# Expert rows in units of 64 (blocks of 256, 384 and 320), with TensorE's loop over pairs of experts written out four times

## What is computed

```python
gate = jnp.einsum('bsd,ed->bse', x, Wg) + routing_bias
_, top_idx = jax.lax.top_k(gate, K)            # K = 4 of E = 8
mask = jax.nn.one_hot(top_idx, E, dtype=gate.dtype).sum(-2)
masked_gate = jnp.where(mask > 0, gate, -jnp.inf)
weights = jax.nn.softmax(masked_gate, axis=-1) * mask
out = _swiglu(x, Ws1, Ws2, Ws3)
h1 = jnp.einsum('bsd,ehd->ebsh', x, W1)
h2 = jnp.einsum('bsd,ehd->ebsh', x, W2)
eo = jnp.einsum('ebsh,edh->ebsd', jax.nn.sigmoid(h1) * h1 * h2, W3)
out = out + jnp.einsum('ebsd,bse->bsd', eo, weights)
```

## Time and profile before

| | us |
|---|---|
| runs shown | 993.48 (median), 991.69, 5251.34 |
| the profiled execution | 993.76 |
| its span in the profile | 992.0 |

### The profile page before, as it was taken

The page is one execution under the profiler, slowest core; times in us unless marked ns, Lnnn a source line. Parts: engine busy times, 40 slices in busy tenths (PEclk is TensorE's granted clock), DMA queues, the critical chain, the costliest instruction groups (busy, mean ns, idle before and its releaser), DMA issues.

```text
span 992.0 us, 25401 instructions
## 1 busy us (share of the span) xinstructions
PE 975.7 (98%) x8054; PEld 798.5 (80%) x8054; DVE 560.8 (57%) x1411; ACT 508.4 (51%) x1250; POOL 545.4 (55%) x513
## 2 busy tenths in 40 slices
PE   9998999999999999999999999999999999999997
PEld 4665666788887888888788878788888887887886
DVE  4998787745544454545444545454455444554686
ACT  3676444355454554455445545445455454554366
POOL 4554027757633347633956016076888880785873
PEclk9999999999999999999999999999999999999999
DMA  6859024355532333353244214218773882785785
GB/s 223 248 143 185 1 60 131 99 173 131 163 108 78 104 92 97 98 171 96 59 145 138 57 48 124 58 49 187 127 101 68 125 132 53 106 127 88 103 149 143
DMA packets 168051, 113.86 MB, mean 115 GB/s; under 512 B 113596, under 2 KB 160191, under 8 KB 166848
## 3 DMA queue, kind: packets, MB, share of 16 engines
q0 software_dynamic: 29808, 58.37, 27.5%
q1 hardware_dynamic: 115888, 33.15, 16.1%
q10 hardware_dynamic: 22304, 21.76, 6.6%
HBM read 47.09 MB, written 43.12 MB: 91 GB/s over the span
## 4 chain that ended last, share of the span: by engine, by line
PE 87%; POOL 5%; DVE 3%; issue 2%; DMA 1%; ACT 1%; SPq 1%; ACTq 0%; DVEq 0%; POOLq 0%
PE psA L1073 53%; PE psB L1104 22%; PE psA L1021 5%; POOL y_sum L759 4%; PE psA L1104 2%; PE psB L1107 2%; DMA y_sum<-rows_by_place,place 1%; PE psC L1055 1%; DVE g_lo L1509 1%; PE psB L1034 1%; PE psC L1048 1%; SPq L519 1%; PE psC L1175 0%; DVE psC L1499 0%; DVE work L1291 0%
## 5 line engine op out<-in xcount | busy, mean ns | idle before, releaser
L874 ACT ACTIVATE sil<-psA 128x256 f32<-128x256 f32 (+1 forms) x456 | 178.3, 398 | 281.6 <-PE psA L1073 253.7
L759 POOL DMA_INDIRECT y_sum<-rows_by_place,place x128 | 200.0, 1563 | 82.5 <-issue 39.0
L1499 DVE SCALAR_TENSOR_TENSOR g<-psA,sil 128x256 f32<-128x256 f32 (+1 forms) x160 | 72.0, 450 | 306.1 <-ACT sil L874 305.7
L1073 PE MATMUL psA<-xb_odd,work 128*128 128x256 f16 x1980 | 221.1, 273 | 0.4 <-issue 0.4
L1073 PEld LDWEIGHTS psA<-xb_odd,work 128*128 128x128 f16 x1980 | 193.0, 98 | 24.1 <-issue 1.4
L1104 PE MATMUL psB<-work,g_hi 128*128 128x256 f16 x1260 | 211.5, 273 | 0.8 <-DVE g_lo L1509 0.3
L1073 PE MATMUL psA<-xb,work 128*128 128x256 f16 x1782 | 199.0, 273 | 2.2 <-issue 1.3
L1073 PEld LDWEIGHTS psA<-xb,work 128*128 128x128 f16 x1782 | 173.4, 98 | 24.4 <-issue 4.0
L1499 DVE SCALAR_TENSOR_TENSOR psC<-psA,sil 128x256 f32<-128x256 f32 (+3 forms) x296 | 133.0, 449 | 77.2 <-ACT sil L874 71.2
L1104 PE MATMUL psB<-work,g_lo 128*128 128x256 f16 x630 | 171.8, 273 | 0.0
L706 POOL DMA_INDIRECT rows_by_place<-y_rows,place x96 | 95.1, 990 | 136.6 <-DMA rows_by_place<-y_rows,place 122.5
(11 more groups left out here) (176 smaller groups left out, 1036.0 us busy)
## 6 DMA issues: line engine op xcount, KB each, us to landing
stage<-wpack POOLq DMA_DIRECT2D x9, 2176.0 KB, 8.9
rows_by_place<-eb ACTq DMA_DIRECT2D x57, 256.0 KB
work<-xT SPq DMA_DIRECT2D x7, 512.0 KB, 6.0
work<-half_beta SPq DMA_DIRECT2D x6, 512.0 KB, 4.6
work<-x_tok POOLq DMA_DIRECT2D x6, 512.0 KB, 6.8
rows_by_place<-eb ACTq DMA_DIRECT2D x6, 384.0 KB
rows_by_place<-zeros SPq DMA_DIRECT2D x1, 2112.0 KB, 12.9
rows_by_place<-y_rows,place POOLq DMA_INDIRECT x128, 2.5
```

What stands on the lines that cost most here:

```text
L759: pool.indirect_dma_start(out=y_sum[:, n, :], out_offset=None, in_=xs, in_offset=bass.IndirectOffsetOnAxis(ap=place[:, k, n:n + 1], axis=0 ...
L874: act.activation(sil[r0:r0 + n, c % SLOTS, 0:T], psA[0:n, chunk_bank(c, T), 0:T], ACT.Silu, scale=1.0 / (XS * WS)).then_inc(silu_ready, 1)
L1073: last = pe.matmul(dst, W[:, ws, k, ci, :], xb[slot][:, KD * xs_ + k, 0:T], start=(k == 0 and n == 0), stop=(k == KD - 1 and n == 2))
L1499: dve.scalar_tensor_tensor(gated_rows(g, c, 0, n, T), src, 1.0 / (XS * WS), sil[r0:r0 + n, c % SLOTS, 0:T], ALU.mult, ALU.mult).then_inc(g ...
```

## The change

Sizes are counted in units of 64 rows. An expert with `u` units (at least 4; from 5 to 11 units it is rounded up to a multiple of 4) is cut as before into an inner loop of 256 blocks, and behind it there can be a block of 384 (`wide`, when bit 1 of `u` is set) and a block of 320 (`short`, when bit 0 is set). The 256 blocks are the units that are left. With the rows above, `u` is 45, 48, 17, 34, 21, 23, 46, 25, in all 259, and the blocks (256 + 384 + 320) are 10+0+1, 12+0+0, 3+0+1, 7+1+0, 4+0+1, 3+1+1, 10+1+0, 5+0+1: 54 of 256, 3 of 384 and 5 of 320. A 320 block moves 384 rows in and out (`J = 3` groups, `-(-T // P)`), has three groups in `down`, and 320 columns in `up`.

```diff
+UNIT = P // 2
+TM = TL - UNIT
...
+        def units_of(eng, units):
+
+            short, wide = eng.snap(units & 1), eng.snap((units >> 1) & 1)
+            return eng.snap(units >> 2), wide, short
...
-            with eng.If(full > 0):
-                with eng.Fori(0, turns) as i:
-                    run(TB, first + 2 * i, rows_from(2 * i), 2 * w)
-                    left = eng.snap(full - 2 * i)
-                    with eng.If(left > 1):
-                        run(TB, first + (2 * i + 1), rows_from(2 * i + 1), 2 * w + 1)
-            with eng.If(odd > 0):
+            with eng.Fori(0, turns) as i:
+                run(TB, first + 2 * i, rows_from(2 * i), 2 * w)
+                left = eng.snap(full - 2 * i)
+                with eng.If(left > 1):
+                    run(TB, first + (2 * i + 1), rows_from(2 * i + 1), 2 * w + 1)
+            with eng.If(wide > 0):
                 run(TL, eng.snap(first + full), None if group is None else eng.snap(group + JB * full), 4 + w)
+            with eng.If(short > 0):
+                run(TM, eng.snap(eng.snap(first + full) + wide),
+                    None if group is None else eng.snap(eng.snap(group + JB * full) + JL * wide), 5 - w)
...
-            with pe.Fori(0, E // 2) as p:
-                counted(pe, weight_set_ready, 2 * p + 1)
-                expert_turns(0, lambda c: read_second(pair_words[0], c))
-                counted(pe, weight_set_ready, 2 * p + 2)
-                expert_turns(1, lambda c: read_first(pair_words[1], c))
-                for p0 in range(E // 2 - 1):
-                    nc.regs_mov(pair_words[p0], pe.snap(pair_words[p0 + 1], min_val=1, max_val=(NT + 1) * FIELD ** 2 - 1))
+            for p in range(E // 2):
+                pe.wait_ge(weight_set_ready, 2 * p + 1)
+                expert_turns(0, lambda c: read_second(pair_words[p], c))
+                pe.wait_ge(weight_set_ready, 2 * p + 2)
+                expert_turns(1, lambda c: read_first(pair_words[p + 1], c) if p + 1 < E // 2 else None)
...
-                t.add(dve.tensor_scalar(cnt_i[:, 0, :], inc[:, :, NT - 1], 1.0, P - 1.0, ALU.mult, ALU.add))
+                t.add(dve.tensor_scalar(cnt_i[:, 0, :], inc[:, :, NT - 1], 1.0, 2.0 * P - 1.0, ALU.mult, ALU.add))
```

128 lines of the change are left out of this document (81 added, 47 removed).

## The result

| | before, us | after, us |
|---|---|---|
| median (7 runs each) | 994.17 | 1002.33 |
| lowest, highest | 991.69, 5251.34 | 997.45, 1008.54 |
| the profiled execution | 993.76 | 1008.54 |
| its span | 992.0 | 1006.8 |

The changed kernel takes 1.0088 times as long as the kernel before, with a 95% interval from 1.0065 to 1.0112: about 8 us more where 9 us less were forecast. The forecast of 985 and its range of 981 to 991 both missed; that the change stays under 2% either way, which had 0.97, came true. The profiled execution is the slowest of the seven. I profiled another execution of the same kernel later, with a span of 1000.0 us (1001.8 us of time, close to the median of 1002.33).

A forecast was written before the change was run, and what follows sets the result against it. PE's columns were taken to bound the experts. Terms of -8.8 (columns), -1.5 (ends of pairs), +1.0 (jumps) and +0.4 (DVE) made -8.9 us: span 992.0 to 983.1, forecast 985, range 981 to 991.

The forecast's parts named there:

- Columns: Experts' up on PE: 5 fewer units of 64 columns at 1.76 us each, down unchanged; -8.8 us.
- rival (a): PE's jumps into new code wait for instruction packets: 1005 us in full (chance 0.03), 990 in part (0.10).
- A jump alone is nearer to the second … I take 0.15 us for each of the 7 new ones: PE's jumps over absent blocks, 12 instead of 5: nearly free as PE's sequencer runs ahead; +1.0 us, bounds 0 and 5.6.
- three double jumps: Where two of PE's jumps follow each other: rival (a) in part, 3 x 1.7 us, giving 990; chance 0.10.
- The shorter chunk should still cover them: 320 block: chunks of 1.63 us against 1.95 still cover DVE and ACT, so up takes 8.96 us.
- Rival (b): 320 blocks cost what 384 blocks do, tied to ACT and DVE: 993.5 us, no gain; chance 0.04.
- Ends of pairs: PE's idle time between pairs of experts shrinks as register moves and branch back go; -1.5 us, bounds 3.84 and no gain.
- DVE in the ahead block: Fourth ahead block: fourteen small DVE operations instead of six delay the rests, so PE waits 0.4 us; +0.4.
- PE meets this only through weights … Cost 0: More zeros and wider loads: PE meets them only through expert 3's weights, with up to 1.6 us covered; cost 0.
- Collisions: Stalls from POOL and DVE working together in the blocks are shuffled, not removed: 0, give or take 1.5 us.
- Rival (c): POOL is late with expert 3's weights by more than the 1.6 us of slack: 987 us; chance 0.10.
- The end moves with PE: Behind the experts: the last gathers still begin 5.3 us behind PE, so the end shifts with it.

The follow-up runs named there:

- e4: The changed kernel with its 320 blocks made 384 columns wide in up and on ACT and DVE; 1008.71 us, 1.0136 times before.
- e6: e2 with 239 never-run instructions of one more 384 block put behind each expert's 384 block on PE and jumped over; 1004.41 us, 1.0117 times before.
- e2: The kernel before, old block sizes kept, with only PE's loop over the pairs of experts written out; 991.09 us, 0.9969 times before.
- e1: The changed kernel's new sizes with PE's loop over the four pairs put back; 1013.8 us, 1.0195 times before.
- e9: e8 with PE's pairs of experts written out instead of looped; 1000.82 us, 1.0051 times before.
- e10: The changed kernel with 78 never-run instructions ahead of expert 0 on PE, shifting the code behind; 1003.02 us, 1.0083 times before.
- e11: e9 with 50 never-run instructions ahead of expert 0 on PE, shifting the code behind; 993.31 us, 0.999 times before.
- e8: The changed kernel with at most one large block an expert, shared down code, ACT's sizes early and PE's pair loop kept; 995.89 us, 1.0018 times before.
- e5: The changed kernel with ACT working out its large-block sizes before its inner loop and holding them in registers; 999.18 us, 1.0057 times before.
- e3: The changed kernel with the code of absent 384 and 320 blocks left out on PE, for these inputs only; 989.46 us, 0.9957 times before.
- e12: The changed kernel again, nothing edited, for one more profiled execution (the second profile); a span of 1000.0 us.

## Why the prediction was wrong

**Columns: right.** -8.8 us were forecast, and the undisturbed lengths of the blocks give -9.0. e4's blocks confirm it from the other side. That PE's columns bound this kernel was right too.

The prediction named what would show rival (a) right: an idle time of 1 us or more at the first matmul behind a jump, with a q8 packet beside it. That is what the trace has. Its condition for being wrong altogether is met too: the stage got longer.

**"A jump alone is nearer to the second … I take 0.15 us for each of the 7 new ones": this step failed.** Two of the twelve jumps cost 6.57 + 5.66 = 12.2 us in the profiled execution and 9.4 in the second profile, and a third place some 2.5 us together with ACT's part. The others cost 0 to 0.4, apart from the one behind which expert 5's load was late. The mechanism was rival (a)'s, which had 0.13 in all, and its range end of 991 came from "three double jumps". Three things in its working were wrong.

First, the evidence against it. The jump before 450.63 had a packet beside it and cost only 0.1 us more than the same jump with the code present. But in narrower windows the packet begins at 450.9 us, after PE had gone on, so it isn't what PE waited for. And that jump went 210 instructions ahead, into code that was there or on its way, and then back to the loop's head, which had run before. It was a short jump, followed by one to code that was there. e6 differs from e2 only in 239 more instructions under that jump, and there it costs 6 us. Rows that show a jump to be cheap say so for its distance and its landing place, not for jumps.

Second, the price. It was taken from how long a packet takes to move, 1.7 us. An idle stretch is 2.3 to 4.8 us (e1's 9.35 apart). At the two of the profiled execution the packet begins 1.2 and 1.1 us after the last matmuls end and takes 1.1 and 0.9 us, and the next matmuls begin 1.8 us after it, so most of the price is ahead of the packet and behind it. Half of the clock comes on top, 1.4 to 2.9 us of `up`. The prediction had no term for the clock at all, although show it at 1.00 through the experts' stage, so there was something to lose.

Third, the count. Neither "all twelve" nor "three double ones" was the rule. What the profiles fit is a rule of position. The code comes in packets of about 250 instructions, and on new code PE has the one it is in and the next. A jump that lands in one of these is nearly free; one that lands beyond, or close to the end of the next, waits. 490 instructions (expert 1) missed in both positions tried; 243 (expert 4) missed in one and not in the other. How well such a rule forecasts is open: e9, e10 and e11 were forecast with it, and all three came out 3 to 5 us beyond their ranges; the prediction only noticed that a jump is "nearly a packet's worth". The Trainium skill, "Runtime: NRT & Kernel Launch", section "Instruction fetch mechanics", states it: a taken branch whose target isn't in the current window of two pages waits for a fetch of the target page. For jumps ahead into new code the runs agree on the two pages, as far as two shifts and the lengths 210, 243 and 490 can show it. For jumps back they don't: the heads of the bodies of 1349 and 1668 instructions lie more than two pages back, and going there fetched nothing (20 and 21 packets in the whole span). The next sentence there says that this is one reason why kernels prefer full unrolling; the prediction called the section one against the unrolling and left that out. Here full unrolling is better only where the body is too long to stay (e1 against the change, 11.5 us), or where only short code is skipped (e2 against the kernel before); for a body that stays, the loop spares the miss from its second turn on (e8 against e9, 4.9 us by the medians, 3.3 by the ratios).

**"The shorter chunk should still cover them": wrong by 0.9 us a block.** In the change a 320 block took 14.21 us from start to start only once, in the second profile, with 8.97 us of `up`. There PE had been held up for 3.6 us ahead of it, so ACT was long ready. In e8, e9 and e11, where ACT has its sizes early and PE comes 0.1 to 1.0 us late, they take 14.21 to 14.44 us. That confirms the line between 256 and 384 as what PE needs. The other 320 blocks of the change take 9.88 to 10.35 us of `up` (expert 4's in the first profile, 10.65, is the clock). The argument compared ACT's busy time with the block's, and the register work isn't in the busy time; it is a delay at one place, the start of the first large block behind an inner loop, where only two chunks are in flight. The change also made it longer, by the sizes of two kinds of large block. Even the 384 blocks, undisturbed before, lost 0.35 and 0.85 us. Together that is 4.1 us, and e5 took back 3. Rival (b) named the coupling of PE to ACT and DVE, but with a full 384's price and with busy times as the only test.

**Ends of pairs: not shown.** -1.5 us were forecast; e2 gave 3.6 us against the kernel before, of which the two ends of pairs can be at most 1.9 (0.99 and 0.88 were lost there). In its profile they still lose 0.2 at expert 1 and 1.3 at expert 5, so they gave only 0.4 us; the whole stage is 2.1 us shorter, and the stages ahead of it and behind it 1.5. In the change expert 1's end became a stall.

**DVE in the ahead block: right, but not all.** The fourth ahead block took 16.49 us, 0.5 more than 15.97 before, where 0.4 was forecast. The fifth took 16.21 in both profiles (15.96 before), for which there was no term. The sixth took 17.52 and in the second profile 16.85 (16.44 before), with PE idle 1.39 and 0.73 us at its end for the load of the first expert block, so more than half of what it lost is that execution's and not the change's.

**"PE meets this only through weights … Cost 0": wrong by 1.1 to 1.6 us.** PE also meets a load directly, ahead of expert 5's 384 block; why it is late is open. With the 1.0 us that this expert's 320 block loses, its new cut, which was to save 1.9 us, costs 0.7 us in the first profile and 0.2 in the second.

**Collisions: 0 ± 1.5 held in one profile and not in the other.** The blocks' small losses were 7.4 us before, of which some 1.9 at the ends of pairs. They were 7.2 and 4.4 after. One of them shows how little decides. Before, DVE's rest began 0.07 us ahead of POOL's conversion and took 0.43 us (first fence); after, it began 0.18 us behind it, and took 1.62 (second):

```profile
654.70 0.43 DVE L1509 TENSOR_TENSOR g_lo<-g,g_hi 128x256 f16<-128x256 f32 x1
...
654.77 1.74 POOL L622 TENSOR_TENSOR work<-stage,work 128x704 f16<-128x704 f32 x1
```

```profile
667.46 1.62 DVE L1552 TENSOR_TENSOR g_lo<-g,g_hi 128x256 f16<-128x256 f32 x1
...
667.28 1.52 POOL L637 TENSOR_TENSOR work<-stage,work 128x704 f16<-128x704 f32 x1
```

PE's block around it took 12.31 us instead of 10.70. This one came in every profile of a kernel with the new sizes (1.60 to 1.62 us) and in none of the old ones (before, e2, e6), so it goes with the new sizes' timing and not with chance.

**Weights of expert 3: right.** PE came to expert 3 some 7 us after 499 us in the change, because of the stalls, and in e3, which has none, at 495.1, as forecast. The 320 block ahead of it has an undisturbed `down` of 5.24 us there. Rival (c) didn't happen.

**"The end moves with PE": nearly.** From the experts' end to the end of the span it was 83.17 us and is 85.45 (85.3 in the second profile). PE waits there for DVE's rests, once for 1.50 us:

```profile
986.72 0.39 PE L1119 MATMUL psB<-wshared,g_hi 128*128 128x256 f16 x2 [1.50 <-DVE g_lo L1552]
```

Why it does so more than before I didn't test.

**The sum.** For the profiled execution: -9.0 for the columns, +12.2 for two missed jumps with their clock, +2.4 at expert 2, +4.1 in the other large blocks, +1.6 for expert 5's late load, -0.2 for all other blocks, +1.4 ahead of them and +2.3 behind: +14.8 us, from 992.0 to 1006.8. For the second profile the two jumps make +9.4, expert 2 +2.7, the other large blocks +4.1, expert 5's late load +1.1, all other blocks -3.0, the stage ahead +0.6 and the one behind +2.1: +8.0, and the span is 1000.0.

## What to carry to other kernels

Where code is skipped on the engine that bounds the kernel, lay its program out in pieces of about 250 instructions and mark what each jump skips: a jump past the next piece, into code that hasn't run, cost some 4 us here, and with the clock's fall about 6, more than the work that a finer choice of block sizes may save. A loop whose body stays on the engine pays this only in its first turn; written-out code can pay at every absent piece; so either keep the choice inside a body that stays, or keep what is skipped short. And a busy share says nothing about what an engine's sequencer does between two instructions: a chain of register work at a block's start is a delay, and it counted here, where only two chunks are in flight. An expectation of the place of a stall should be checked in more than one profiled execution, since the same kernel ran with and without the clock's fall.

## What the runs showed of the hardware that I had not expected

- **A missed jump on PE**: 2.3 to 4.8 us idle, all but one of them 3.6 or more, put down in the matmul's row to the load of a later block or (e8, e1) to "issue". A q8 packet stands inside the idle time (in the shortest, e4's second, and in e1's of 3.92 us it begins some 0.4 us ahead of it). The profiles of after, e4, e5, e6, e8, e9, e10 and e12 hold fourteen such stretches; e1 has three more, of 3.92, 3.09 and 9.35 us, the last with packets of q8 at two times.
- **The clock**: at fifteen of these seventeen stretches the granted clock fell from 1.00 to 0.50, sometimes only when PE had resumed, and it rose again 3 to 6 us after the matmuls had resumed. Twice it didn't fall (642.05 in the second profile, 3.58 us idle; 733.88 in e1, 3.09 us). In the experts' stage it didn't fall at the idle times of up to 1.5 us. That isn't general: in the recurrent stage of the kernel before, where PE runs short groups of matmuls with idle times between, it fell inside an idle time of only 0.69 us:

```profile
88.00:89.00 1.00, 0.36 (x1) 0.13 (x2) 0.94 (x4) 0.00 (x0) 0.92 (x2) 0.70 1.23 61
89.00:90.00 1.00, 1.00 (x4) 0.41 (x3) 0.96 (x3) 0.39 (x1) 0.89 (x3) 0.50 1.38 197
```

- **A loop body on PE**: 1349 and 1668 instructions stayed (20 and 21 packets in the whole span), 1846 didn't (48 packets).
- **Code that never runs isn't free**: 239 instructions under a condition that never holds cost 13.3 us of 991 (e6), and 50 such instructions in another place gained 7.5 us in the medians (e11 against e9).
